# One GNN layer over 100,000 nodes: a 512-column memset behind every third row gather in place of a 256-column memset behind each

## What is computed

```
h = jnp.maximum(_layernorm(x, axis=-1), 0.0)
edge_in_f = jnp.concatenate([h[src], h[dst], edge_attr], axis=-1)
agg  = segment_sum(mlp2(edge_in_f, W1_f, b1_f, W2_f, b2_f), dst)
edge_in_r = jnp.concatenate([h[dst], h[src], edge_attr], axis=-1)
agg += segment_sum(mlp2(edge_in_r, W1_r, b1_r, W2_r, b2_r), src)
out = x + h + mlp2(jnp.concatenate([agg, h], axis=-1), Wn1, bn1, Wn2, bn2)
```

## Time and profile before

| what | us |
|---|---|
| median of the runs (three, 1625.42 to 1633.73) | 1631.61 |
| the profiled execution, its own time | 1627.22 |
| span of that execution in the trace | 1625.50 |
| GpSimd busy in the span | 1120.1 (69%) |
| VectorE busy in the span | 972.4 (60%) |
| TensorE busy in the span | 1318.5 (81%) |

### The profile page before, as it was taken

The page is one execution under the profiler, slowest core; times in us unless marked ns, Lnnn a source line. Parts: engine busy times, 40 slices in busy tenths (PEclk is TensorE's granted clock), DMA queues, the critical chain, the costliest instruction groups (busy, mean ns, idle before and its releaser), DMA issues.

```text
span 1625.5 us, 29085 instructions
## 1 busy us (share of the span) xinstructions
PE 1318.5 (81%) x7070; PEld 997.1 (61%) x7070; DVE 972.4 (60%) x2902; ACT 944.0 (58%) x2256; POOL 1120.1 (69%) x1003
## 2 busy tenths in 40 slices
PE   6988998457787788887877887878888865899998
PEld 4777776345565666665656665656666654666665
DVE  7999998336666666666665666666666641222222
ACT  5888888244555455555545555455555533677776
POOL 7899878888888888888888888888888862000000
PEclk9999999567878777778787778787777777999999
DMA  7999998335555555555545555555555546999998
GB/s 222 310 312 315 315 312 280 101 59 108 103 109 108 107 104 103 102 103 103 102 93 99 101 103 102 98 100 102 103 103 102 102 76 205 333 369 348 346 349 292
DMA packets 238374, 280.71 MB, mean 173 GB/s; under 512 B 53170, under 2 KB 155200, under 8 KB 238348
## 3 DMA queue, kind: packets, MB, share of 16 engines
q1 hardware_dynamic: 168408, 241.57, 44.7%
q0 software_dynamic: 68992, 38.59, 20.3%
q10 hardware_dynamic: 948, 0.30, 0.1%
HBM read 162.62 MB, written 117.72 MB: 172 GB/s over the span
## 4 chain that ended last, share of the span: by engine, by line
POOL 28%; issue 19%; DMA 15%; PE 9%; DVE 5%; ACT 1%; POOLq 0%; SPq 0%; DVEq 0%; another core or an unknown queue 0%; ACTq 0%
POOL table L532 24%; DMA out_x<-ncentred 12%; POOL got_odd L514 5%; DMA table<-to_send,scatter_at 3%; PE bank L846 3%; DVE ncentred L1137 2%; PE bank L820 2%; PE bank L818 2%; PE bank L833 1%; DVE same L979 1%; PE bank L871 1%; DMA same<-table 1%; PE bank L804 1%; PE bank L882 0%; DVE sums L961 0%
## 5 line engine op out<-in xcount | busy, mean ns | idle before, releaser
L532 POOL DMA_INDIRECT table<-to_send,scatter_at x392 | 640.9, 1635 | 134.1 <-issue 118.3
L846 PEld LDWEIGHTS bank<-message,same 128*128 128x128 f32 x1960 | 300.1, 243 | 47.1 <-issue 43.6
L846 PE MATMUL bank<-message,same 128*128 128x128 f32 x1960 | 322.4, 335 | 3.3 <-DVE message L1010 3.3
L639 ACT ACTIVATE nh<-nx,all_sums,all_rstd 128x64 f32<-128x64 f32 x784 | 280.2, 434 | 0.0
L514 POOL DMA_INDIRECT got_even<-in_x,gather_first x196 | 211.8, 1081 | 40.9 <-issue 36.1
L775 PE MATMUL bank<-wn_h,nturned 128*128 128x256 f32 x784 | 196.6, 394 | 26.9 <-ACT nhidden L683 18.4
L514 POOL DMA_INDIRECT got_odd<-in_x,gather_at x180 | 179.9, 999 | 54.8 <-issue 54.2
L818 PE MATMUL bank<-turned,w_ends 128*128 128x256 f32 x392 | 175.5, 540 | 37.8 <-ACT turned_edge L609 37.1
L804 PE MATMUL bank<-ident,h_ends 128*128 128x128 f32 x196 | 51.4, 355 | 184.4 <-DVE h_ends L1019 181.4
L1004 DVE TENSOR_TENSOR scatter_at<-moved,ids 128x4 int32<-128x4 f32 x98 | 16.0, 163 | 296.6 <-DMA table<-to_send,scatter_at 296.6
L775 PEld LDWEIGHTS bank<-wn_h,nturned 128*128 128x128 f32 x784 | 143.1, 192 | 63.3 <-issue 33.0
(11 more groups left out here) (78 smaller groups left out, 1971.0 us busy)
## 6 DMA issues: line engine op xcount, KB each, us to landing
nx<-in_x SPq DMA_DIRECT2D x194, 256.0 KB
table<-nhidden SPq DMA_DIRECT2D x97, 512.0 KB
same<-table SPq DMA_DIRECT2D x97, 512.0 KB, 5.3
others<-numbers SPq DMA_DIRECT2D x196, 128.0 KB
out_x<-ncentred SPq DMA_DIRECT2D x97, 256.0 KB, 4.4
nx<-out_x SPq DMA_DIRECT2D x55, 256.0 KB, 4.6
out_x<-nh SPq DMA_DIRECT2D x31, 256.0 KB
table<-to_send,scatter_at POOLq DMA_INDIRECT x392
```

What stands on the lines that cost most here:

```text
L532: pool.indirect_dma_start(table, bass.IndirectOffsetOnAxis(ap=scatter_at[s][:, k:k + 1], axis=0), to_send[s][:, k, :], None, compute_op=AL ...
L639: last = act.activation(nh[s][:, g, :], nx[place][:, g, :], ACT.Relu, bias=all_sums[:, at, g:g + 1].rearrange("p a g -> p (a g)"), scale=a ...
L846: last = pe.matmul(bank[6 + s][:, k * M:(k + 1) * M], same[s][:, o, k * P:(k + 1) * P], message[s][:, o, :], start=(o == k), stop=(o == KB ...
```

## The change

A gather that isn't a third one goes straight on to the next gather. Behind every third one stands one memset, and it covers all 512 columns of `to_send[0]`. There are 208 early gathers, so 69 memsets in place of 208, and one gather stands behind the last memset. ScalarE's wait is for 69 (`KB * (PAIRS + LOOK) // TRIO`) in place of 208.

```diff
+    TRIO = 3
...
-        idle = to_send[0][:, 0:2, :].rearrange("p k m -> p (k m)")
+        idle = to_send[0][:, 0:4, :].rearrange("p k m -> p (k m)")
...
-            pauses = 0
+            pauses = taken = 0
...
                         gather(got_odd[i][:, 0, :], at, s_got[i], [k])
                     else:
                         continue
+                    taken += 1
+                    if taken % TRIO:
+                        continue
                     if pauses:
                         pool.wait_ge(s_paused, pauses)
                     pool.memset(idle, 0.0).then_inc(s_paused, 1)
...
                 elif s == 0:
-                    act.wait_ge(s_paused, KB * (PAIRS + LOOK))
+                    act.wait_ge(s_paused, KB * (PAIRS + LOOK) // TRIO)
```

## The result

| | kernel before | changed kernel |
|---|---|---|
| median, us | 1629.58 (four runs, 1625.42 to 1633.73) | 1757.43 (four runs, 1723.28 to 1784.57) |
| profiled execution, us (span) | 1627.22 (1625.50) | 1765.86 (1764.1) |
| last early gather begins, us | 338.0 | 310.71 |
| first scatter begins, us | 340.86 | 474.65 |

The changed kernel is slower: 1.065 times the time before, interval 1.051 to 1.080. The forecast was 1627. Ratios here and further down leave out runs that are over 1.5% above the fastest of their kernel, two of the changed one's four; its median over all four is 1.078 times the one before.

A forecast was written before the change was run, and what follows sets the result against it. Every engine was taken to wait for the last memset of the early gathers; 4.8 us gained there less 0.3 at the end made 4.5, taking the median from 1631.61 to 1627, range 1614 to 1634.

The forecast's parts named there:

- The sequence of gathers: GpSimd's 208 early gathers with their memsets: undisturbed, 69 trios make 291.3 us against 300.4, 9.1 us less.
- quiet trio: Three early gathers, their gaps and one memset, with nothing disturbing: 4.22 us, against 4.33 for three gathers before.
- The holds: Early gathers begun inside a two-SBUF-input VectorE instruction wait for its end, then need 0.83 us: 30.5 us instead of 26.3.
- The one long gap: A single odd gap of 4.72 us among the early gathers, its cause not shown; kept in the forecast, 4.56 us extra.
- held less: Rival, chance 0.22: trios fall between VectorE's multiplies in the begin loop; around 14 us gained, up to some 31, time 1618.
- What costs nothing: Begin loop: the wider memset and as many gathers as before cost 0; 56 us from 283 to 339 cover it.
- Locked on two windows: Rival, chance 0.08: a gather of each trio always held by VectorE, each trio 5.35 us; 17 us later, 1649.
- The rule that spoke against the change: Begin loop: VectorE multiplies begun inside a gather wait half of 0.957 us on average, about 2.5 us more; time 1634.

The follow-up runs named there:

- 1.395: Quiet time per gather, in us, of the changed kernel with a memset of 192 columns behind each gather instead; ratio 1.0185 to the kernel before.
- 1.42: Quiet time per gather, in us, of the changed kernel with a memset of 224 columns behind each gather instead; ratio 0.998 to the kernel before.

## Why the prediction was wrong

**The sequence of gathers: right, and its sizes nearly.** Gaps of 0.30 and 0.16, a memset of 0.542 (0.539 taken), 0.95 for a gather behind a gather (0.977 taken): a quiet trio is 4.17 instead of 4.22.

**The holds: the rule stood, its input did not.** The 28 held gathers of the changed kernel's early part end 0.82 or 0.83 us behind VectorE's instruction, as reckoned. But 30.5 us were reckoned with VectorE's multiplies where they had been. Of the gathers' 210.9 us only 12.9 are above 208 x 0.952, because VectorE did a third of its work, and 189 gathers instead of 171 had begun by 283 us. The one long gap came to 2.69 us, not 4.72. The last memset therefore ended at 310.54, and not at 334.0. A sequence this short was in the prediction's own "held less", down to 308; it was reckoned a gain of 14 us.

**"What costs nothing" is the step that failed.** It said that the begin loop shares its time with as many gathers as before, so that it costs nothing, with 56 us of cover. The number of gathers was indeed not what changed; the time between them was. While gathers come faster than one in 1.40 us, TensorE's results come late. The kernel before leaves 1.445 at the least, and its holds make the mean 1.60; the change goes to 1.39, and the begin loop's last window began 174 us later, three times its cover. By 4.22 the trio would have stood at 1.407, between the 1.395 that loses time and the 1.42 that doesn't; whether the 0.05 us between the trio forecast and the one measured, which are nothing in the sum, decided the outcome, no run shows. Once the begin loop falls behind, VectorE holds fewer gathers and they come faster, so the starving would feed itself. That would explain the spread of the changed kernel's runs too, but only one of them has a trace, so it is argued and not shown. At 208 us of the profiled run GpSimd paused 2.69 us of its own, and the begin loop then ran near its full pace for a while (6, 7, 5, 4 windows in each 20 us from 220 us on, 0 to 2 from 40 to 200 us).

**The rivals.** None had this cause. "Locked on two windows" was slower as well, but by 17 us and for a hold that did not occur. The rule that spoke against the change, by which gathers hold VectorE's multiplies, has nothing to do with it: the multiply's longest is 0.731 us (0.719 in the earlier trace rows). Its 1634 also added 2.5 us of begin loop to the time whole, which the 56 us of cover would have hidden.

**What stays open.** What the serial thing is. All the times here come from executions that the profiler recorded, and records of semaphores are missing from the traces in the begin loop, most where gathers run closely (of ScalarE's 459 updates from 20 to 270 us the trace of before holds 216, of its 41 in the run without memsets 8). The Trainium skill's "NOTIFIC — the notification-queue block", section "The write path", says that this block's internal pipeline holds its producers back rather than lose a record. By that rule the recording itself may be what queues, and then the loss may be absent where nothing is recorded. No run here shows an execution without it, and none shows the block's state. That TensorE's waits take no turn, that SyncE's issues become longer, and that ScalarE's and VectorE's instructions take no turn that the traces show, is unexplained as well.

## What to carry to other kernels

An instruction that does nothing can be what keeps a stream below the pace that something else can take. Before thinning out such pauses, find the interval that the stream keeps now, and look for what runs beside it at a fixed interval; a cost that is hidden by "as much work as before" holds only at the pace of before. Where a wait is put down to nothing in the trace, halve and double what is waited for, and see whether the wait goes with it.

## What was not expected of the hardware

- GpSimd's indirect gathers closer than 1.40 us apart make TensorE's results known late: 28 us after the transposes (162.03 to 189.88 in the run without memsets), where the kernel before needs 1.2 (100.46 to 101.64).
- The lateness counts loads and multiplies: 1.40 us each (24, 16 and 32 of them in 33.7, 22.4 and 44.9 us), satisfied waits nothing.
- It outlasts the gathers: TensorE is late until 300 to 302 us where 208 gathers, 1.288 us apart in the mean, end at 275.4. With 416 gathers of 64 rows GpSimd itself is held, to 1.41 in the mean from 200 us on.
- SyncE's issue of a load takes 0.73 instead of 0.34 us meanwhile.
- A gather of 64 rows takes GpSimd 0.91 us, one of 128 rows 0.95.
